# A transformer kernel's first dense network, from four-pass float32 products to three single-pass products of split operands, with GpSimd's residual sums cut by token tile

## What is computed

```python
def _L0_attn_ref(x, ln1_g, ln1_b, Wqkv, bqkv, Wo, bo, ln2_g, ln2_b, W1, b1, W2, b2):
    ...
    attn = jax.nn.softmax(scores, axis=-1)            # 16 heads of 16, causal
    attn_out = jnp.einsum('bhqk,bhkd->bhqd', attn, v)
    ...
    x = x + (attn_out @ Wo + bo)
    h = _layer_norm(x, ln2_g, ln2_b)
    h = jax.nn.gelu(h @ W1 + b1, approximate=False) @ W2 + b2     # 256 -> 1024 -> 256
    return x + h
...
    h = h + _L0_attn_ref(_layernorm(h), ...)          # layer 0, with the network above
    h = h + _L0_ffn_ref(_layernorm(h), ...)           # ternary weights, 256 -> 1024 -> 256
    h = h + _L1_attn_ref(_layernorm(h), ...)          # 16 heads of 64, 4 key/value heads
    h = h + _L1_ffn_ref(_layernorm(h), ...)           # 8 experts, 2 per token, fixed capacity
```

## Time and profile before

| quantity | value |
|---|---|
| median of 3 runs | 1863.71 us |
| the profiled execution's own time | 1864.7 us |
| its span, first to last instruction | 1862.9 us |
| PE busy | 1720.3 us, 92% |
| DVE busy | 1255.3 us, 67% |
| ACT busy | 970.3 us, 52% |
| POOL busy | 693.1 us, 37% |
| mean granted clock of PE | 0.958 |

### The profile page before, as it was taken

How to read it: one execution, slowest core, us unless ns; L and a number is a source line. 1 busy time by engine, 2 the same in 40 slices (tenths; PEclk the granted TensorE clock), 3 DMA queues, 4 the chain that set the end, 5 groups by cost and what they waited for, 6 DMA issues and landing times.

```text
span 1862.9 us, 33716 instructions
## 1 busy us (share of the span) xinstructions
PE 1720.3 (92%) x11231; PEld 1413.5 (76%) x11231; DVE 1255.3 (67%) x4074; ACT 970.3 (52%) x2670; POOL 693.1 (37%) x1084
## 2 busy tenths in 40 slices
PE   4687999999999999899999999974999999999997
PEld 3465777777767677678887788853898999899896
DVE  6578778787778675858777878767755445444542
ACT  1356657575667667656667777620334333333421
POOL 2251434324242421433444445430534524533431
PEclk8688999999999999999999999985899999999998
DMA  7112010101011010101011110021232321122210
GB/s 215 40 38 66 1 64 3 62 10 55 10 38 60 2 35 2 35 23 48 27 35 35 35 35 27 2 80 33 92 102 66 109 91 62 39 81 68 65 41 22
DMA packets 74245, 91.04 MB, mean 49 GB/s; under 512 B 16523, under 2 KB 64310, under 8 KB 74072
## 3 DMA queue, kind: packets, MB, share of 16 engines
q1 hardware_dynamic: 61464, 67.90, 11.2%
q0 software_dynamic: 9472, 16.77, 3.2%
q10 hardware_dynamic: 3136, 4.21, 0.7%
HBM read 71.02 MB, written 25.00 MB: 52 GB/s over the span
## 4 chain that ended last, share of the span: by engine, by line
PE 65%; issue 13%; DVE 8%; POOL 5%; POOLq 3%; ACT 2%; DVEq 1%; DMA 1%; SPq 0%; ACTq 0%
PE bank L1618 17%; PE bank L1049 12%; PE bank L1633 10%; PE bank L997 6%; PE bank L979 6%; PE bank L1032 5%; PE bank L1214 3%; PE bank L1076 2%; DVE probs L2322 1%; POOLq L3190 1%; POOL rot L3216 1%; POOL rstd_b L3191 1%; ACT probs L1746 1%; DVE at_least L2963 1%; POOLq L3213 1%
## 5 line engine op out<-in xcount | busy, mean ns | idle before, releaser
L1746 ACT ACTIVATE probs<-probs,nmax 128x128 f32<-128x128 f32 (+2 forms) x768 | 381.0, 500 | 64.3 <-DVE nmax L2322 62.8
L997 PE MATMUL bank<-cst,probs 128*128 128x128 f32 x1536 | 237.4, 284 | 20.7 <-ACT probsT L1754 9.9
L3254 POOL TENSOR_SCALAR probs<-probs,rowsum 128x128 f32<-128x128 f32 (+2 forms) x384 | 179.1, 486 | 194.9 <-DVE rowsum L2338 194.7
L997 PEld LDWEIGHTS bank<-cst,probs 128*128 128x128 f32 x1536 | 177.4, 144 | 65.7 <-issue 27.1
L1618 PE MATMUL bank<-xeT,gate_w 128*128 128x480 f32 x768 | 187.7, 380 | 0.5 <-issue 0.5
L1618 PE MATMUL bank<-xeT,up_w 128*128 128x480 f32 x768 | 187.3, 380 | 0.0
L3126 DVE TENSOR_TENSOR prod<-bank,sil 128x480 f32<-128x480 f32 x128 | 84.1, 657 | 147.9 <-PE bank L1618 147.0
L1633 PE MATMUL bank<-down_w,hT 128*120 128x256 f32 x1536 | 181.3, 280 | 0.0
L1633 PEld LDWEIGHTS bank<-down_w,hT 128*120 128x120 f32 x1536 | 179.9, 182 | 0.1
L1754 ACT COPY probsT<-bank 128x384 f32<-128x384 f32 x256 | 120.8, 472 | 105.2 <-PE bank L997 90.6
L2470 DVE COPY probsT<-bank 128x384 f32<-128x384 f32 x256 | 141.6, 553 | 40.6 <-PE bank L997 35.8
(11 more groups left out here) (363 smaller groups left out, 3566.3 us busy)
## 6 DMA issues: line engine op xcount, KB each, us to landing
gate_raw<-in_L_ffn_gate_w SPq DMA_DIRECT2D x8, 1024.0 KB, 4.8
up_raw<-in_L_ffn_up_w SPq DMA_DIRECT2D x8, 1024.0 KB, 6.9
down_raw<-in_L_ffn_down_w SPq DMA_DIRECT2D x8, 1024.0 KB, 5.7
img<-in_x SPq DMA_DIRECT2D x8, 768.0 KB, 5.1
residual_rows<-x SPq DMA_DIRECT2D x8, 384.0 KB, 2.5
residual_rows<-h_in SPq DMA_DIRECT2D x8, 384.0 KB, 3.6
xr<-residual_rows SPq DMA_DIRECT2D x8, 384.0 KB, 4.6
hr<-residual_rows SPq DMA_DIRECT2D x8, 384.0 KB, 3.9
```

The source lines that it names most:

```text
L997: last = tr(ps[bank][:, P * q:P * (q + 1)], probs[:, n % 4, SEG[t] + P * j:SEG[t] + P * (j + 1)], ident)
L1746: last = f(p, p, ACT.Exp, bias=nmax[:, n % 4, t:t + 1], scale=-1.0, accum_out=rowsum[:, where, t:t + 1])
L3254: last = g.tensor_scalar(p, p, rowsum[:, n, t:t + 1], 1.0, ALU.mult, ALU.mult)
```

## The change

Weights and activations of the first dense network are split. Once, in `U_FIRST`, ACT copies `w1` and `w2` in fp32r (`mlp_weights_upper`) and DVE subtracts (`mlp_weights_lower`, 4096 columns). In every unit with `k.s2`, `take_mlp` is now four ACT instructions (upper and raw, two halves; DVE's part is gone), `gelu(m)` is two ACT instructions (upper into `hid_parts`, raw into `hid_raw`), and GpSimd makes the lower parts (`x_lower`, `hidden_lower`, 128x384 each, ten per image). `mlp_up(m)` is six products of 384 columns, `mlp_down(t)` 24 products of 256 columns. Each residual sum on GpSimd is three instructions of 256 columns. The orders of all engines are rewritten, in layer 1 too. To make room, the descriptor memory of GpSimd's own transfers is 2048 bytes.

```diff
@@ TensorE
-                            taken(sec, i, "lnM0", "lnM1")
-                        product(sec, i, f"up0_{m}", [(w1[:, c, P * m:P * (m + 1)], xTb[:, c, :]) for c in range(DC)], S)
+                            pe.wait_ge(mlp_split, 1)
+                            pe.wait_ge(mlp_x_split, at(s2_img, DC, DC))
+                        product(sec, i, f"up0_{m}", [piece for c in range(DC) for piece in (
+                            (w1_hi_block(c, m), x_parts[:, 0, c, :]), (w1_hi_block(c, m), x_parts[:, 1, c, :]),
+                            (w1_lo[:, c, P * m:P * (m + 1)], x_parts[:, 0, c, :]))], S)
...
-                            taken(sec, i, *[f"up0_{m}" for m in range(FM)])
-                        token_major(sec, i, "down0", t, hidT, w2, FM)
+                            pe.wait_ge(mlp_hid_split, at(s2_img, FM, FM))
+                        cols_t = slice(P * t, P * (t + 1))
+                        product(sec, i, f"down0_{t}", [piece for m in range(FM) for piece in (
+                            (hid_parts[:, 0, m, cols_t], w2_hi[:, m, :]), (hid_parts[:, 0, m, cols_t], w2_lo[:, m, :]),
+                            (hid_parts[:, 1, m, cols_t], w2_hi[:, m, :]))], D)
@@ ScalarE
-                        ln_affine(sec, i, "lnM0", xTb[:, 0, :], 4, 6)
+                        for c in range(DC):
+                            banks.wait_filled(act, sec, f"lnM{c}", i)
+                            f(x_parts[:, 0, c, :], ps[banks.bank(sec, f"lnM{c}")][:, 0:S], ACT.Identity,
+                              bias=cols[:, 6 + c:7 + c], scale=cols[:, 4 + c:5 + c])
+                            ln_affine(sec, i, f"lnM{c}", x_raw[:, c, :], 4 + c, 6 + c)
...
-                        take(sec, f"up0_{m}", i, hidT[:, m, :], ACT.Gelu, S, bias=cols[:, 4 * DC + m:4 * DC + m + 1])
+                        bias = cols[:, 4 * DC + m:4 * DC + m + 1]
+                        banks.wait_filled(act, sec, f"up0_{m}", i)
+                        f(hid_parts[:, 0, m, :], ps[banks.bank(sec, f"up0_{m}")][:, 0:S], ACT.Gelu, bias=bias)
+                        take(sec, f"up0_{m}", i, hid_raw[:, m, :], ACT.Gelu, S, bias=bias)
@@ ScalarE and VectorE, in U_FIRST
+                    mlp_weights_upper()
...
+                    mlp_weights_lower()
@@ GpSimd
+                def by_tiles(dst, src, bias_row):
+                    for t in range(NT):
+                        last = g.tensor_tensor(dst[:, t, :], src[:, t, :], bias_row, ALU.add)
+                    return last
...
-                        g.tensor_tensor(x1[:], x1[:], row(bo_r), ALU.add).then_inc(resid_made, 1)
+                        by_tiles(x1, x1, bo_r).then_inc(resid_made, 1)
...
+                def hidden_lower(m):
+                    if k.s2:
+                        banks.wait_taken(pool, sec, f"up0_{m}", i)
+                        g.tensor_tensor(hid_parts[:, 1, m, :], hid_raw[:, m, :], hid_parts[:, 0, m, :].bitcast(F32), ALU.subtract) \
+                            .then_inc(mlp_hid_split, 1)
...
-                        g.tensor_tensor(xr[:], hr[:], row(bf2_r), ALU.add).then_inc(resid3_ready, 1)
+                        by_tiles(xr, hr, bf2_r).then_inc(resid3_ready, 1)
...
-                    ffn_residual()
                     deviation(LN_ATTN0, 2)
                     residual_x()
+                    ffn_residual()
                     residual_h()
@@ the program
-    nc = bacc.Bacc("TRN2", target_bir_lowering=False, num_devices=1)
+    nc = bacc.Bacc("TRN2", target_bir_lowering=False, num_devices=1, dynamic_dma_scratch_size=2048)
```

More of the change, by code:

```diff
@@ L446, in early_fusion_kernel @@
         rinv = sb("rinv", [P, NT, P])
+        rinvT_start = offsets["top"]
         rinvT = sb("rinvT", [P, S])
@@ L1275, in unit @@
                     norm_second()
+                    turn(3, 1)
                     turn(4, 0)
@@ L1294, in unit @@
                     mlp_up(3)
+                    scores(5)
+                    turn(6, 0)
                     mlp_up(4)
-                    scores(5)
                     mlp_up(5)
-                    turn(6, 0)
                     turn(6, 1)
@@ L1407, in unit @@
                     mix(3)
-                    mlp_up(7)
-                    turn(9, 0)
-                    turn(9, 1)
-                    second_queries(0)
-                    mlp_down(0)
-                    scores(6)
+                    second_queries(0)
+                    turn(9, 0)
+                    mlp_up(5)
+                    turn(9, 1)
+                    scores(6)
+                    mlp_up(6)
+                    mlp_up(7)
                     norm_moe()
@@ L3282, in mlp_residual @@
                         pool.wait_ge(resid_loaded, at(s2_img, 16, 16))
-                        g.tensor_tensor(hr[:], hr[:], xr[:], ALU.add).then_inc(resid2_ready, 1)
+                        for t in range(NT):
+                            last = g.tensor_tensor(hr[:, t, :], hr[:, t, :], xr[:, t, :], ALU.add)
+                        last.then_inc(resid2_ready, 1)
                 def ffn_residual():
@@ L3326, in unit @@
                     deviation(LN_MLP, 2)
+                    scale(4)
+                    x_lower(0)
                     deviation(LN_MOE, 0)
-                    scale(4)
+                    x_lower(1)
                     scale(5)
+                    scale(6)
                     deviation(LN_ATTN1, 2)
                     deviation(LN_MOE, 1)
-                    scale(6)
-                    deviation(LN_MOE, 2)
+                    hidden_lower(0)
                     scale(7)
+                    hidden_lower(1)
+                    hidden_lower(2)
                     scale(8)
```

358 lines of the change are left out of this document (201 added, 157 removed).

## The result

The changed kernel takes 1885.76 us, the median of 4 runs (1884.05 to 1886.01), beside 1864.01 for the kernel before on the same chip: a ratio of 1.011, 95% interval 1.0089 to 1.013. The forecast was 1851.5.

The account below looks back on a forecast made before the run. PE was taken to set the time of nearly every stage. Products -25, residual sums -6, ACT +10, lower halves +5, first unit +4 and reordering 0 gave -12: 1852.7, or 1851.5 on the median's scale; range 1833 to 1868.

Parts of the forecast that it names:

- Products, second GELU, first unit's weights: Layer 0: cheaper split products on PE -25 us, ACT's second GELU per block +10, splitting weights in the first unit +4.
- The waits of 0.85 and 0.35 us: Up phase: PE stands before blocks 5 and 6 for ACT's GELUs, 1.2 us an image, +10 us in all.
- All is given back: Rival: ACT sets the up phase, new waits of 27 us cancel the gain, 1860 to 1867; chance 0.12.
- Residual sums by tile: GpSimd's sums in three pieces block DVE less, ending PE's 1.42 us wait in loop units; -6 us (0 to -9).
- First unit: ACT copies and DVE subtracts 4096 weight columns once, most of it showing; +4 us (bounds 0 and +9).
- Small memory: GpSimd's indirect transfers in the experts: no term; waiting for each landing would cost 70 us, held very unlikely.
- Lower halves: GpSimd's ten lower halves per image delay DVE's stack subtractions: 0.6 us an image, +5 us (bounds 0 and +20).
- Two of them blocked ... a third of that reaching PE: Of DVE's six `stack_lower(0)` subtractions two blocked for most of 0.98 us, a third reaching PE: 0.6 us an image.
- The rest of the reordering: New order of all engines, layer 1 and units 6 to 8 included: PE's work the same, 0 us (-6 to +6).
- The slower rival: Rival: GpSimd and DVE alternate at the first stack, 4.9 us an image, 34 us more, 1886; chance 0.13.

Follow-up runs that it names:

- `tiles_scratch`: The kernel before with only the residual sums in three pieces and the 2048-byte descriptor memory; 1849.6 us.
- `order_only`: The changed kernel's order, sums by tile and small memory, with the old float32 products, single GELUs and no lower halves; 1878.3 us.
- `no_lower`: The changed kernel without GpSimd's eight lower halves of the hidden columns, the third down product taking the upper half instead; 1866.5 us.
- `new_dve`: The changed kernel with the edge image's norms back ahead of the hidden blocks and all ten lower halves on VectorE; 1870.5 us.
- `old_order`: Split products on the kernel before's order, with sums by tile and small memory, all lower halves on VectorE; 1867.7 us.
- `order_norm`: `order_only` with VectorE's norms of the edge image back ahead of the second network's hidden blocks; 1869.3 us.
- `queue`: The changed kernel with one GpSimd call, the deviation for the norm ahead of the stack, moved before the first hidden lower half; 1881.6 us.
- `old_pool`: `old_order`, but with GpSimd instead of VectorE making the eight lower halves of the hidden columns; 1881.1 us.

## Why the prediction was wrong

By medians the change is a walk of four steps: 1864, less 14 for tiles and memory (`tiles_scratch`), plus 29 for the order (`order_only`), less 12 for the products with the second GELU, the input's lower halves and the weights (`no_lower`), plus 19 for GpSimd's lower halves: 1886. The steps aren't independent; on the old order the products with all they need cost 18. The time left the range by one step, the order: with it at its upper bound, +6, and all else as measured it would have been 1863, inside.

- *Products, second GELU, first unit's weights: -25 + 10 + 4 = -11 forecast, -12 measured.* Twelve up products take 2.19 us (385.75 to 387.94), 24 down products 2.95 (404.43 to 407.38), as worked out. PE's busy time in a loop unit is 80.7 us at full clock (`new_dve`, `old_order`), where about 80 was forecast. The waits of 0.85 and 0.35 us forecast for blocks 5 and 6 are 0.60 and 0, the second hidden behind the stack's. It fits partly by luck: on the old order the second GELU with VectorE's lower halves costs 21, and that kernel (1867.7) comes near to the rival "All is given back" (1860 to 1867).
- *Residual sums by tile, -6: right.* -7.5 alone; in the changed kernel the wait fell to 0.42.
- *First unit, +4: about right.* It takes 8.6 us more, of which 5.3 are the order's (82.5 in `order_only`, 79.2 in `order_norm`) and 3.3 come with the rest, the split of the weights above all (85.3 in `no_lower`).
- *Small memory, 0 with a slower price held unlikely:* it gains 6, in the tail behind the last scatter, which I had not looked at.
- *Lower halves, +5 (bounds 0 and +20): mis-sized,* 19 measured, just inside the bounds. "Two of them blocked ... a third of that reaching PE" is the step that failed. The three `stk_q` subtractions alone lost 2.5 us, the norm ahead of them another 0.7 and 1.95 of queue. 1.6 us of it reached PE, without cover, since the stack was already 1.2 us late (1.16 to 2.72). Over four loop units PE waits 1.4 us a unit more than in `no_lower`, and is busy 1.1 us more with the same products, at a lower clock: 2.5 us a unit and not 0.6.
- *"The rest of the reordering. PE's work is the same ... I take 0 (bounds -6 and +6)": failed,* 29 measured. This step decided the result. PE's work was the same, but who meets whom wasn't. The embedding's new place stood in the order that I quoted, and I took its time from the trace of before, without putting it on a time axis against the up products; and I did not ask for the second network what the moved norm lets GpSimd start, nor what that collides with.
- *The clock* stood in no term. Waits cost TensorE its clock behind them, in some units and not in others.

How much is clock can be estimated from four loop units at once: before, changed, and `new_dve`, which has the split products at full clock (windows):

```profile
246.99:589.97 342.98, 332.31 (x2163) 255.45 (x2162) 272.91 (x901) 221.10 (x642) 122.40 (x204) 1.00 0.10 33
258.53:613.71 355.18, 330.23 (x2321) 269.55 (x2321) 278.85 (x897) 242.57 (x685) 176.57 (x277) 0.98 0.10 32
253.00:598.48 345.48, 322.76 (x2322) 263.28 (x2322) 285.66 (x938) 242.96 (x686) 138.51 (x236) 1.00 0.10 33
```

PE's idle time grows from 2.7 to 6.2 us a unit, 3.6 more. Its busy time would be 80.7 us at full clock, 2.4 less than before, and is 82.6. So of the 3.05 us a unit, an estimate from these rows is +3.6 for waits, +1.9 for the clock behind them and -2.4 for the products.

The slower rival gave 1886, and its place was right: `stk_q` behind lower halves. Its price was not: 2.5 us a loop unit and not 4.9. The lower halves cost 19 us and not the 39 it gave them; what was missing came from the order, of which it said nothing. That its time was hit is luck.

Left open: the cause of the last 8 of the order's 29 us, nearly all of it in the loop units (1.5 us each), of which two small waits show a part; and why one wait is followed by half clock and another of the same length is not.

## What to carry to other kernels

Where an edit comes with a rewritten order, put the moved instructions of every engine on one time axis from the trace of before, and ask of each what it now releases and what that runs beside; "the same work" is no bound. Take a change's parts one by one on the old order first: here two small parts gain 14 us, and the part that gave the change its name costs 18 in the best of the places tried. A cheaper product pays only as far as the engine that prepares its operands keeps pace.

## What the runs showed of the hardware

- Nearly the same waits can cost some 3 us more or less by the clock (`queue`: 87.30 us at 1.00, 90.32 at 0.96, neighbouring units of one kernel, with PE busy 2.9 us longer in the second). Not every wait does it: `old_pool` stood 2.4 us in front of its stack with the unit's clock at 1.00. The run-to-run spread goes with it: the kernel before took 1861.6 us at a mean clock of 0.961 and 1875.4 at 0.951.
- From the issue of the last indirect transfer to the program's end passed 10.9 us with the default descriptor memory (two kernels) and 3.7 to 4.2 with 2048 bytes (18 kernels). What fills that time is not shown.
- A GpSimd subtraction of 384 columns takes 1.00 us. Three VectorE subtractions of 256 columns take 3.51 us beside such ones, 1.06 before the change and 1.10 with GpSimd held back. On VectorE a subtraction of 384 columns takes 0.55 us.
